# One DVE step moved in the cross-attention loop: a turn now follows the next mask pass

## What is computed

```python
q = (text_hidden @ Wq)      # 16 heads of 128
k = (vision_tokens @ Wk)    # 8 key heads, each shared by 2 query heads
v = (vision_tokens @ Wv)
scores = einsum('bhtd,bhsd->bhts', q, k) / scale
scores = where(mask, scores, -inf)
attn = softmax(scores, axis=-1)
out = einsum('bhts,bhsd->bhtd', attn, v)
return out @ Wo
```

## Time and profile before

| | before |
|---|---|
| median of three runs | 375.74 us |
| the profiled execution | 377.27 us |
| its span, first to last instruction | 375.5 us |
| PE busy | 343.1 us (91%) |
| DVE busy | 286.7 us (76%) |
| POOL busy | 244.6 us (65%) |
| ACT busy | 226.5 us (60%) |
| mean granted TensorE clock | 0.973 |

### The profile page before, as it was taken

One profiled execution on the slowest core, in us unless ns is written; L12 is line 12 of the kernel. 1 busy time (PEld: TensorE's weight loads), 2 busy tenths in 40 slices (PEclk: granted clock), 3 DMA queues, 4 the chain that ended last, 5 costly groups with the idle time before them and its releaser, 6 DMA issues.

```text
span 375.5 us, 6913 instructions
## 1 busy us (share of the span) xinstructions
PE 343.1 (91%) x2240; PEld 308.1 (82%) x2240; DVE 286.7 (76%) x481; ACT 226.5 (60%) x402; POOL 244.6 (65%) x150
## 2 busy tenths in 40 slices
PE   4886689998999999999999998996989999898996
PEld 1765578997997997997998887996988897698995
DVE  3489968987987987987987977535457745769997
ACT  2468487677686685685685677642035455246772
POOL 4917499699679579579669579464234843746550
PEclk9999999999999999999999999997599999969999
DMA  7504885877777777778668668842016011133640
GB/s 214 201 2 112 203 202 131 214 177 169 179 171 168 183 166 174 183 160 180 155 147 182 161 145 210 220 138 84 2 33 192 0 57 58 28 101 106 178 134 29
DMA packets 33332, 52.07 MB, mean 139 GB/s; under 512 B 5792, under 2 KB 23328, under 8 KB 33312
## 3 DMA queue, kind: packets, MB, share of 16 engines
q1 hardware_dynamic: 33168, 51.56, 54.9%
q10 hardware_dynamic: 144, 0.26, 0.4%
HBM read 20.08 MB, written 0.26 MB: 54 GB/s over the span
## 4 chain that ended last, share of the span: by engine, by line
PE 74%; DVE 12%; issue 5%; SPq 2%; DMA 2%; ACT 2%; POOL 2%; DVEq 0%; ACTq 0%
PE bank L536 12%; PE bank L537 11%; PE bank L538 11%; PE pair L536 10%; PE pair L538 10%; PE pair L537 10%; SPq L261 2%; PE bank L776 2%; DVE probs L1304 2%; DVE blocks L1315 1%; DVE xn L1242 1%; PE pair L732 1%; DMA resid<-in_x_dram 1%; PE pair L768 1%; PE pair L762 1%
## 5 line engine op out<-in xcount | busy, mean ns | idle before, releaser
L408 POOL TENSOR_TENSOR pT<-pT,pT_hi 128x1024 fp32r<-128x1024 f32 x60 | 142.6, 2406 | 40.7 <-ACT pT_hi L1013 40.5
L1003 ACT ACTIVATE probs<-probs,lowest 128x2048 f32<-128x2048 f32 x32 | 64.3, 2009 | 45.0 <-DVE lowest L1304 45.0
L536 PE MATMUL bank<-pT_hi,ctx_lo 128*128 128x256 f32 x240 | 68.2, 284 | 1.1 <-POOL pT L408 1.1
L537 PE MATMUL bank<-pT,ctx_hi 128*128 128x256 f32 x240 | 68.7, 286 | 0.0
L538 PE MATMUL bank<-pT_hi,ctx_hi 128*128 128x256 f32 x240 | 68.1, 284 | 0.0
L1013 ACT ACTIVATE pT_hi<-pT 128x1024 fp32r<-128x1024 f32 x60 | 61.5, 1050 | 10.1 <-DMA pT<-blocks 9.0
L536 PE MATMUL pair<-ctxT_hi,qk_lo 128*128 128x512 f32 x128 | 51.6, 403 | 6.2 <-DVE lowest L1304 2.3
L538 PE MATMUL pair<-ctxT_hi,qk_hi 128*128 128x512 f32 x128 | 50.1, 391 | 0.0
L537 PE MATMUL pair<-ctxT_lo,qk_hi 128*128 128x512 f32 x128 | 50.0, 391 | 0.0
L536 PEld LDWEIGHTS bank<-pT_hi,ctx_lo 128*128 128x128 f32 x240 | 45.3, 189 | 2.5 <-POOL pT L408 1.5
L537 PEld LDWEIGHTS bank<-pT,ctx_hi 128*128 128x128 f32 x240 | 45.1, 188 | 1.0
(11 more groups left out here) (230 smaller groups left out, 857.8 us busy)
## 6 DMA issues: line engine op xcount, KB each, us to landing
pT<-blocks SPq DMA_DIRECT2D x128, 128.0 KB, 2.3
pT<-ctx_raw SPq DMA_DIRECT2D x112, 128.0 KB, 2.3
ctx_raw<-ffn_experts_gate_up_dram SPq DMA_DIRECT2D x16, 256.0 KB, 3.1
wq<-in_L_xattn_Wq_dram SPq DMA_DIRECT2D x8, 256.0 KB, 2.9
wo<-in_L_xattn_Wo_dram SPq DMA_DIRECT2D x8, 256.0 KB, 3.0
blocks<-in_L_attn_w_q_dram SPq DMA_DIRECT2D x4, 512.0 KB, 4.0
blocks<-in_L_attn_w_dense_dram SPq DMA_DIRECT2D x4, 512.0 KB, 4.0
ctx_raw<-_L_ffn_experts_down_dram SPq DMA_DIRECT2D x16, 128.0 KB, 2.6
```

The source lines that it names most:

```text
L408: pool.tensor_tensor(dst, src, hi.bitcast(F32), ALU.subtract).then_inc(ready, 1)
L536: pe.matmul(dst, w[1], x[0], start=start, stop=False)
L537: pe.matmul(dst, w[0], x[1], start=False, stop=False)
L1003: act.activation(probs[:, j], probs[:, j], ACT.Exp, bias=lowest[:, p, j, 1:2], scale=-1.0, accum_out=den[:, p, j:j + 1]).then_inc(exps, 1)
```

## The change

In `group(g)` of the DVE, pass 4 (the first pass of the second unit) and turn 1 (the second row of the first unit) change places. Pass 4 then stands directly behind turn 0, on whose count it waits (`turned` at least 4g + 1), and turn 1 directly behind pass 4. It holds for groups 1 to 7; group 0, the prologue, keeps its order.

```diff
                 mask_pair(g, 3)
                 turn(g, 0)
+                mask_pair(g, 4)
                 turn(g, 1)
-                mask_pair(g, 4)
                 if out_on:
                     add_out(2 * (g - 2) + 1, 2 * (g - 2) + 1, 1)
                 denominators(2 * (g - 1) + 1, 1)
```

## The result

Over 20 runs each, the changed kernel takes 379.19 us in the median and the kernel before 376.02; the ratio is 1.0068 with a 95% interval of 1.005 to 1.0085. That is 2.6 us (1.9 to 3.2) on 376. One of the changed kernel's 20 runs took 425.1 us at a granted clock of 0.749, a slow state of the chip, and stands outside of the ratio. The two medians are 3.2 us apart, at the upper end of that interval.

The account below looks back on a forecast made before the run. A ring through DVE, ACT and PE's y projection was taken to bound the cross-attention loop; handoffs of 0.75 and 0.09 plus landings of 1.21 and 0.42 gave 2.5 us, 378.2 us on a median of 375.74, range 376.4 to 380.1.

Parts of the forecast that it names:

- The ring sets the period: Cross-attention loop: a ring through DVE, ACT and PE's y projection without slack sets the 27.94 us a group.
- Pass 4 earlier gives nothing: DVE, pass 4 ahead of turn 1: its reader, score 6, doesn't start sooner in the loop; gain zero.
- Handoff, 0.10 us behind turn 0 and 0.16 us a group: DVE, groups 2 to 6: pass 4 waits for turn 0 directly in front; rounded 0.15 a group, 0.75 us in all.
- the rival of a free handoff: DVE, pass 4 behind turn 0: the semaphore costs nothing, only the later turn 1 does; 377.1 us, chance 0.07.
- the prediction's division: DVE, pass 4's start behind turn 0: 0.10 us in the loop with register thresholds, 0.03 us with constants.
- Group 2, 1.21 us: Head of group 2: the first unit's later landing has no cover and delays the ring once by 1.21 us.
- The rival that the late landing costs nothing: Landing of the first unit, group 2: only the handoff costs; 376.7 us, chance 0.12.
- Group 7, 0.42 us: Head of group 7: landing 1.27 us later against a cover of 0.85 us, so 0.42 us lost.
- Groups 3 to 6 are covered with 0.44 us left: DVE's remainder before pass 1: the oT_hi copy, 1.27 us later, still ends 0.44 us ahead of it; cost zero.
- The sum: Whole kernel: loop handoffs 0.75, group 7's handoff 0.09, landings 1.21 and 0.42, together 2.5 us more, 378.2 us.
- the likeliest case: Whole kernel: handoffs plus late landings in groups 2 and 7; 378.2 us, spanning 377.6 to 379.3, chance 0.62.
- Two rivals: Late landing costs nothing: 376.7 us, chance 0.12; cover fails in groups 3 to 6, 0.4 us each: 379.9, chance 0.08.

Follow-up runs that it names:

- v1: Kernel before, with DVE's oT remainder for the y projection ahead of pass 5 and ACT's yT_hi copy ahead of the last rounding; 0.9856, 5.4 us less.
- e3: Kernel before, order kept, but pass 4 waits for the count of turn 1, directly in front, instead of turn 0; 1.0034, 1.3 us more.
- e1: Kernel before, with pass 4 ahead of turn 1 in group 1 alone; 1.0025, 0.9 us more.
- v1a: v1 with the swap of turn 1 and pass 4 on top; 0.9975 against the kernel before, 4.5 us more than v1.

## Why the prediction was right, step by step

- *The ring sets the period.* Right: v1 shows it. The loop went from 27.96 to 26.98 us by two changes of order on DVE and ACT, with PE's instructions the same.
- *Pass 4 earlier gives nothing.* Right. PE's wait in front of the y projection grew; nothing came earlier.
- *Handoff, 0.10 us behind turn 0 and 0.16 us a group.* The mechanism is right, and the rival of a free handoff fell with e3. That the size came out so near is partly luck. The start is 0.13 us behind the turn's end, and the step to the sums 5.81 us, 0.21 more than before and not 0.16; the 0.04 us that the first sum gives back, which the prediction didn't have, brought it to 0.15 to 0.16 a group. And the row that the 0.10 was read from does not show what a threshold in a register costs. In group 7 of the kernel before, which is written out with constants, the reciprocal stands as far behind the sums, 226.41 - 226.31:

```profile
225.31 1.00 DVE L1334 SCALAR_TENSOR_TENSOR resid<-bank,rden,resid 128x256 f32<-128x256 f32 x2
226.41 0.17 DVE L1279 RECIPROCAL rden<-den 128x2 f32<-128x2 f32 x1
```

For the pass itself the prediction's division holds. In groups 1 and 7 of the changed kernel it starts 0.03 us behind the turn, as in rows 7 (group 7 below), and in groups 2 to 6 0.13. In the loop a pass also has one wait more, for `mask_ready`; no run separates that from the registers.

```profile
221.95 2.31 DVE L1315 STREAM_TRANSPOSE blocks<-probs 128x2048 f32<-128x2048 f32 x1
224.29 1.22 DVE L1304 CUSTOM_DVE_ANT_0 probs<-pair,mask_bias 128x1024 f32<-128x1024 f32 x1
```

- *Group 2, 1.21 us.* The wait on ACT grew by 1.18 us and DVE's by 1.19. The distance grew by 1.35, for I had told the growth between groups 1 and 2 as 1.1 us and left out group 2's own handoff there; the sum had both. The rival that the late landing costs nothing fell with e1. What I had not seen is the scatter: in the second profiled execution of after DVE waits 1.93 us.
- *Group 7, 0.42 us.* It was 0.23 us of waiting, 0.32 us by DVE's start (215.34 against 213.10, with the pass 0 in front at 212.40 against 210.48). I counted the handoff of group 6 twice, once in the ring and once in the landing's delay of 1.27 us; it delays DVE's arrival as much as the landing, so that the landing is late by only 1.1 us against the ring.
- *Groups 3 to 6 are covered with 0.44 us left.* No wait in either profiled execution. In group 3 of the changed kernel the copy of `oT_hi` ends at 101.94 and DVE comes to it at 102.58, so 0.64 us was left, and in group 4, from which the 0.44 was worked out, 0.67. Most of the difference is the same double count. It shows on ACT too: the landing wait in groups 3 to 6 is 1.44 to 1.65 us over both executions, where 1.7 to 1.8 was told. v1a shows how near the end of this cover is.
- *The sum.* 2.5 us foretold, 2.36 in the traces up to group 7, 2.6 (1.9 to 3.2) in the runs. 378.2 us was worked out on a median of 375.74; the 20 runs of before have 376.02, and those of after 379.19, inside the likeliest case's 377.6 to 379.3. That the first trace comes within 0.14 us is luck in part, for the scatter of one landing is larger than that, and the second pair of traces gives 3.27. Two rivals were priced 0.1 us too high (0.75 + 0.09 on 375.74 is 376.6, four times 0.4 on 378.2 is 379.8), which changes nothing.
- *Open.* What makes one of the 16 issues long, and how often it falls which way. The two pairs of traces, 2.36 and 3.27 us, show how much hangs on it.

## What to carry to other kernels

Before moving a step on an engine that is a quarter idle, follow the ring from one iteration to the next: if the step lies on it, each handoff between neighbours is paid in every iteration, though its engine's busy share doesn't change. For every transfer that hangs on the moved step, work out the cover (arrival of the engine that needs it minus the landing) in the first and the last iteration as well as in the steady one, with delays that the ring itself gets counted on both sides. And cover is not a property of the transfer: a change that makes the period shorter takes it away, as v1 did.

## What the runs showed of the hardware

A mask pass of 128 x 1024 float32 that waits for the turn directly in front of it starts 0.12 to 0.13 us behind the turn's recorded end in the hardware loop, where its thresholds are in registers, and 0.03 us behind it in the groups with constants; it starts 0.08 us ahead of that end when it waits for nothing recent. This holds in all groups of all kernels here that have such a wait. SP issues a transfer of 128 KB from `blocks` to `pT` about every 0.63 us. In the first pass of its loop one of the first unit's 16 took 1.3 to 1.9 us in 11 of the 13 profiled executions, and none over 0.6 in the other two (e1's first and v1a); the 16 took 10.31 to 11.64 us, so that one landing scatters by up to 1.3 us. And the granted clock of the stages behind cross-attention differed between two executions of the same code there, 0.76 and 0.82 in one, 0.80 and 1.00 in another, enough to hide 1.4 us of the loss from a comparison of two spans.
